# Spreading the reciprocal RMS by two DMAs through DRAM, and reordered scatters and stage changes, in a graph layer with a mixture of experts

## The chip, the cores and the metric

The kernel runs on one core of a Trainium2 chip. All data are 32-bit floats in and out. The metric is the device time of the whole program in microseconds (us). PE is TensorE (matmuls and transposes), DVE is VectorE, ACT is ScalarE, POOL is GpSimd, and SP is the engine that here only issues DMAs and waits. Every engine works through its own list of instructions strictly in order, and the engines wait for each other through semaphores.

## The reference

There are 8192 tokens (128 graphs of 64 nodes) of width 128. The first layer aggregates over a graph, the second is a mixture of 8 experts of which each token uses 2:

```
x = x + gnn(layernorm(x), adj)
    agg = epsilon * h + adj @ h
    z   = agg @ W1 + b1                       # 128 -> 512
    z   = silu(z * rsqrt(mean(z*z) + 1e-6) * rms_weight)
    out = z @ W2 + b2                         # 512 -> 128
x = x + ffn(layernorm(x))
    logits = h @ Wg + bg; the two largest, softmax over the two
    out = sum over the two experts e of  w_e * (gelu(h @ W1[e] + b1[e]) @ W2[e] + b2[e])
```

## The kernel before

The work has two stages. The **first stage** goes over 16 groups (G) of 512 tokens, each with its tokens along the free dimension in four pieces (JT = 4) of 128. In its step s PE multiplies group s by W1 (first_layer, L600), adds the skip path (residual, L607) and multiplies by W2 (second_layer, L614), and between these it does work for groups ahead: agg for group s+3 (aggregate, L566), and a quadratic form that gives the mean square of z without computing z (quadratic, L574, the product on DVE, L851, and sum_squares, L582). The mean square of group s+1 leaves DVE (mean_square, L855) at the start of step s, and POOL raises it to the power -1/2 together with two variances (pow_step, L435). The result has one token per partition, four columns. Agg has a feature per partition and tokens along the free dimension. So PE transposes the four columns, each broadcast to 128 columns, into a PSUM bank (spread, L592), where each token's factor then stands in all 128 partitions, and DVE multiplies agg by that bank (scale_agg, L861) in the same step s, ahead of the first layer of group s+1.

DVE also takes the results of the step before out of PSUM (take_x2, L867), makes the second layer norm's statistics, the gate's logits, the two best experts (gate_scores to gate_choice, L890 to L912) and, from prefix sums that PE makes (prefix, L623 to L628), the row of each token in a table per expert (rank_rows, place_rows, L921 to L937). POOL scatters the tokens' rows into these tables in DRAM with one indirect DMA per 128 tokens and choice (dispatch, L446): 64 for the first choices, 64 for the second.

The **second stage** goes over 142 tiles of 128 slots, 71 of first choices and then 71 of second choices. SP loads a tile's rows into a ring of 16 buffers once the tile 16 places earlier has been written (load_slots, L358), DVE normalises it (norm_slots, L1052) and copies its expert's first-layer block (copy_block, L1046), PE transposes it and does both layers (turn, layer1, layer2, L686, L693, L708), ACT does the Gelu (L797), DVE adds bias and weight (finish, L1121), and POOL writes the rows to their tokens: plain writes for first choices (L458), accumulating ones for second choices (L461). The scatters that are left from the first stage stand between the writes on POOL. SP also writes 16 blocks of padding rows (pad, L351), each after reading its place from a table.

The order on every engine is written out by hand. PE's order in a step and DVE's around the changed part are:

```
first_layer(s); residual(s,0); residual(s,1); second_layer(s,0); spread(s+1)          # PE
second_layer(s,1); ...; quadratic(s+2); ...; prefix(s-1); aggregate(s+3); sum_squares(s+2)
take_x2(s-1); stats2_of; moments2_of; mean_square(s+1); norm1(s+3); place_adj(s+4)    # DVE
stats1_of(s+5); gate_scores(s-1); gate_top; scale_agg(s+1); gate_index; gate_choice
product(s+2); rank_rows(s-1); place_rows(s-1)
```

## Time and profile before

| | us |
|---|---|
| median of 3 runs | 490.04 (488.69 to 491.08) |
| the profiled execution, whole | 489.22 |
| its span, first to last instruction | 487.3 |
| PE busy | 468.2 |
| POOL busy | 357.5 |
| DVE busy | 352.8 |
| ACT busy | 263.5 |

The span is what the profile covers; the whole execution has about 1.9 us around it. A busy time is the sum of an engine's instructions; issuing a DMA from SP or waiting is not counted. A timeline row gives start and duration in us, engine, source line, operation, tiles as out<-in with shapes, the number of merged instructions, and in brackets the engine's idle time before the row and what ended it; "issue" means that nothing which the profile shows was waited for. The first stage ends at about 199 us: the last matmuls of its 16th step start at 198.77.

### The profile page before, as it was taken

Reading aid. Unit: us, or ns where it says so; the run is one execution under the profiler, and the core shown is the slowest. Engines: PE = TensorE matmul, PEld = TensorE weight load, DVE = VectorE, ACT = ScalarE, POOL = GpSimd, SP = SyncE. Lnnn points to the kernel's source line nnn. Section 1 sums busy time; section 2 is a strip of 40 time slices with the busy share of each in tenths; the row PEclk is TensorE's granted clock in tenths of the full one; section 3 lists DMA queues with packets and bytes.
Section 4 is the critical chain, followed back from the end, with each engine's and each line's share of the span. In section 5 each row is a group of like instructions: output and inputs, shape, how many; then the busy total and the mean of one; then the engine's idle time right before and its main releaser. Section 6 shows DMA issues by size and latency. Waiting matters only on the chain. (4 is left out here: it accounts for less than half of the span.)

```text
span 487.3 us, 14189 instructions
## 1 busy us (share of the span) xinstructions
PE 468.2 (96%) x3715; PEld 423.1 (87%) x3715; DVE 352.8 (72%) x1476; ACT 263.5 (54%) x829; POOL 357.5 (73%) x318
## 2 busy tenths in 40 slices
PE   8999999999999999799999899999999999999990
PEld 5687888877888877799999799999999999999990
DVE  6788888887887675698866576766767676776751
ACT  2333333333333324477777577777777777777770
POOL 4622577787877777777777777777588888888884
PEclk9999999999999999999999999999999999999997
DMA  5995122222222212332343343333254555555430
GB/s 178 363 316 178 57 72 79 73 77 62 67 68 65 78 45 65 84 80 85 97 113 107 97 112 86 86 89 91 44 69 68 73 72 73 72 69 71 55 33 6
DMA packets 54436, 44.78 MB, mean 92 GB/s; under 512 B 9506, under 2 KB 46024, under 8 KB 54360
## 3 DMA queue, kind: packets, MB, share of 16 engines
q1 hardware_dynamic: 36480, 26.11, 20.3%
q0 software_dynamic: 16592, 17.13, 17.5%
q8 instruction: 35, 0.57, 0.5%
q10 hardware_dynamic: 1288, 0.62, 0.5%
q14 instruction: 41, 0.34, 0.3%
HBM read 25.49 MB, written 19.25 MB: 92 GB/s over the span
## 5 line engine op out<-in xcount | busy, mean ns | idle before, releaser
L797 ACT ACTIVATE gelu_t<-ps,block_w 128x128 f32<-128x128 f32 x568 | 162.0, 368 | 35.9 <-PE ps L693 35.4
L446 POOL DMA_INDIRECT dispatched_rows<-payload,row_idx x128 | 124.9, 976 | 37.4 <-issue 35.9
L693 PE MATMUL ps<-slot_t,block_w 128*128 128x128 f32 x1136 | 150.7, 275 | 0.9 <-ACT gelu_t L797 0.4
L708 PE MATMUL ps<-experts,gelu_t 128*128 x1136 | 150.4, 275 | 0.4 <-ACT gelu_t L797 0.4
L693 PEld LDWEIGHTS ps<-slot_t,block_w 128*128 128x128 f32 x1136 | 138.1, 192 | 1.9 <-issue 0.8
L708 PEld LDWEIGHTS ps<-experts,gelu_t 128*128 128x128 f32 x1136 | 138.2, 192 | 0.8 <-issue 0.8
L461 POOL DMA_INDIRECT out_y<-y_out,slot_rows x71 | 112.6, 1585 | 24.6 <-issue 24.6
L458 POOL DMA_INDIRECT out_y<-y_out,slot_rows x71 | 72.0, 1015 | 23.7 <-issue 18.8
L1121 DVE TENSOR_TENSOR y_bias<-ps,block_w 128x128 f32<-128x128 f32 x142 | 41.4, 291 | 65.3 <-PE ps L708 63.5
L1046 DVE COPY block_w<-experts 128x644 f32 x142 | 73.0, 514 | 1.3 <-issue 1.3
L614 PE MATMUL ps<-w2e,hidden 128*128 128x136 f32 x512 | 69.6, 279 | 0.0
L1052 DVE TENSOR_SCALAR slot_n<-slot_rows 128x128 f32<-128x128 f32 x142 | 58.6, 414 | 8.1 <-DMA slot_rows<-dispatched_rows 7.9
L614 PEld LDWEIGHTS ps<-w2e,hidden 128*128 128x128 f32 x512 | 63.9, 190 | 0.0
L757 ACT ACTIVATE hidden<-ps,vec_cols 128x512 f32<-128x512 f32 x64 | 44.0, 687 | 32.8 <-PE ps L600 32.7
L791 ACT COPY slot_t<-ps 128x128 f32<-128x128 f32 x142 | 37.6, 265 | 40.7 <-PE ps L686 40.2
L600 PE MATMUL ps<-agg_r,w1b 128*128 128x512 f32 x128 | 59.1, 603 | 0.0
L435 POOL TENSOR_TENSOR powers<-powers_in,neg_half 128x12 f32<-128x12 f32 (+2 forms) x17 | 33.8, 1985 | 23.3 <-DVE powers_in L855 22.1
L600 PEld LDWEIGHTS ps<-agg_r,w1b 128*128 128x128 f32 x128 | 23.0, 190 | 22.6 <-issue 22.5
L686 PE MATMUL ps<-ident,slot_n 128*128 128x128 f32 x142 | 38.9, 275 | 3.3 <-DVE slot_n L1052 3.3
L770 ACT ACTIVATE agg<-ps,ones 128x512 f32<-128x512 f32 x16 | 11.0, 687 | 52.4 <-PE ps L566 52.4
L1131 DVE TENSOR_SCALAR y_out<-y_bias,slot_rows 128x128 f32<-128x128 f32 x71 | 31.1, 438 | 2.5
L607 PEld LDWEIGHTS ps<-ident_wg,xs_t 128*128 128x128 f32 x128 | 20.5, 190 | 13.9 <-issue 13.9
(146 smaller groups left out, 416.7 us busy)
## 6 DMA issues: line engine op xcount, KB each, us to landing
slot_rows<-dispatched_rows SPq DMA_DIRECT2D x142, 66.5 KB
xs<-in_x SPq DMA_DIRECT2D x16, 256.0 KB, 5.9
xs_t<-in_x_t SPq DMA_DIRECT2D x16, 256.0 KB, 3.1
experts<-in_f_w SPq DMA_DIRECT2D x16, 256.0 KB, 5.2
out_y<-y_out,slot_rows POOLq DMA_INDIRECT x142, 3.2
adj_in<-in_adj_t SPq DMA_DIRECT2D x16, 128.0 KB, 4.3
dispatched_rows<-payload,row_idx POOLq DMA_INDIRECT x128, 2.5
dispatched_rows<-pad_rows SPq DMA_DIRECT2D x18, 66.5 KB
```

The source lines that it names most:

```text
L446: pool.indirect_dma_start(rows[k], bass.IndirectOffsetOnAxis(row_idx[:, g, j * TOP_K + k:j * TOP_K + k + 1], 0), payload[:, g * JT + j, 0: ...
L458: pool.indirect_dma_start(out, token, y_out[:, r, :], None, bounds_check=T - 1, oob_is_err=False).then_inc(added[r], 16)
L461: pool.indirect_dma_start(out, token, y_out[:, r, :], None, bounds_check=T - 1, oob_is_err=False, compute_op=ALU.add).then_inc(added[r], 16)
L600: pe.matmul(bank(n % H_BANKS, 0, GROUP), w1b[:, c * P:(c + 1) * P], agg_r[:, s % 2, :], start=True, stop=True).then_inc(h_done, 1)
L614: mm = pe.matmul(x2_part(j), hidden[:, c, j * P:(j + 1) * P], w2e[:, c, :], start=False, stop=(c == C - 1))
L693: mm = pe.matmul(bank((2 * i + c // 2) % FH_BANKS, c % 2 * SLOTS, SLOTS), block_w[:, i % BLOCKS, c * P:(c + 1) * P], slot_t[:, i % 2, :], ...
L708: mm = pe.matmul(bank(Y_BANK + i % 2, 0, P), gelu_t[:, i % 2, c, :], experts[:, bass.ds(at + (OW2 + c * P), P)], start=(c == 0), stop=(c = ...
L757: act.activation(hidden[:, c, :], ps[:, (C * s + c) % H_BANKS, :], ACT.Silu, scale=vec_cols[:, GRW + c:GRW + c + 1]).then_inc(hidden_ready, 1)
L797: act.activation(gelu_t[:, i % 2, c, :], ps[:, (2 * i + c // 2) % FH_BANKS, c % 2 * SLOTS:(c % 2 + 1) * SLOTS], ACT.Gelu, bias=block_w[:, ...
L1046: dve.tensor_copy(block_w[:, i % BLOCKS, :], experts[:, bass.ds(at, OW2)]).then_inc(block_ready, 1)
L1052: dve.tensor_scalar(slot_n[:, i % (AHEAD + 1), :], row[:, X2:WID], row[:, MEAN:MEAN + 1], row[:, RSTD:RSTD + 1], ALU.subtract, ALU.mult).t ...
L1121: dve.tensor_tensor(y_bias[:, i % 2, :], ps[:, Y_BANK + i % 2, 0:P], block_w[:, i % BLOCKS, OB2:OB2 + P], ALU.add).then_inc(y_chain, 1)
```

## The change

1. For groups 3 to 15 PE's spread is gone. SP, once the powers are there, stores the four columns (128 partitions x 16 B) in a 2 KB row in DRAM, waits for it, and loads that row into all 128 partitions of `rrms_all` (a part of the tile y_out, which the first stage does not use otherwise). scale_agg then reads both operands from SBUF, the factors with a stride of four elements. PE's quadratic form from group 4 on waits for the product before it instead of for the scaled agg.
2. Second choices on POOL: 2 or 3 in turn per step of the first stage instead of 3, and 3 per five tiles of the second stage instead of 2.
3. POOL no longer waits for all written tiles in one place ahead of the accumulating part, but for two at a time from tile 63 on.
4. The padding blocks on SP: 8 over the last 16 early tiles (every second one), 8 over later tiles (every third), instead of 16 on 16 consecutive tiles.
5. The first four adjacency blocks are placed by DVE instead of POOL.
6. At the end of the first stage DVE normalises two tiles and copies one expert's block earlier, and ACT loads the Gelu table in step 15.
7. ACT's first two DMAs change places.

```diff
+        rrms_all = y_out[:, 2 * JT:, :].rearrange("p (b j) q -> p b (j q)", b=2)
...
-        SECONDS_LEFT = 3 * (G + 1 - SECONDS_FROM)
+        def second_of(s):
+            return (5 * (s - SECONDS_FROM) + 1) // 2
+        SECONDS_LEFT = second_of(G + 1)
...
+            def spread(g):
+                sp.wait_ge(agg_r_ready, g - 1)
+                sp.wait_ge(powers_ready, g)
+                sp.dma_start(rrms_rows[g % 2].rearrange("(p j) -> p j", j=JT),
+                             powers[:, g - 1, 0, :]).then_inc(rrms_stored, 16)
+                sp.wait_ge(rrms_stored, 16 * (g - SPREAD_FROM + 1))
+                sp.dma_start(rrms_all[:, g % 2, :],
+                             rrms_rows[g % 2:g % 2 + 1, :].to_broadcast([P, GROUP])).then_inc(rrms_spread, 16)
+
             for g in range(XT_RING, G):
+                if g - 3 >= SPREAD_FROM:
+                    spread(g - 3)
...
             for i in range(RING, EARLY):
                 load_slots(i)
-                if i == EARLY - KE:
+                if i == EARLY - 2 * E:
                     sp.wait_ge(ends_ready, 1)
-                if i >= EARLY - KE:
-                    pad(i - (EARLY - KE))
+                if i >= EARLY - 2 * E and i % 2 == 0:
+                    pad((i - (EARLY - 2 * E)) // 2)
...
             for i in range(EARLY, TILES):
                 load_slots(i)
+                if i % 3 == 0 and (i - EARLY) // 3 < E:
+                    pad(E + (i - EARLY) // 3)
+            sp.wait_ge(padded, 16 * (KE + TOP_K))
...
-                n = SECONDS_LEFT + (i - 1) // 5 * 2 + (i % 5 == 3)
-                if i % 5 in (1, 3) and n < G * JT:
+                n = SECONDS_LEFT + i // 5 * 3 + i % 5 // 2
+                if i % 5 in (0, 2, 4) and n < G * JT:
                     second(n)
+                if TILES - 8 <= i < TILES - 1:
+                    wait_written(2 * i - TILES)
+                    wait_written(2 * i - TILES + 1)
                 if i == TILES:
-                    for q in range(RING):
-                        pool.wait_ge(added[q], 16 * len(range(q, TILES, RING)))
+                    wait_written(TILES - 2)
+                    wait_written(TILES - 1)
...
-                if g > 1:
+                if 1 < g <= SPREAD_FROM:
                     pe.wait_ge(agg_r_ready, g)
+                if g > SPREAD_FROM:
+                    pe.wait_ge(prod_ready, g)
...
-                if live(s + 1):
+                if s + 1 < SPREAD_FROM:
                     spread(s + 1)
...
+                if s == G - 1:
+                    act.activation(table_warm[:], ones[:, 0:1], ACT.Gelu)
...
+                    dve.wait_ge(rrms_spread, 16 * (g - SPREAD_FROM + 1))
+                    dve.tensor_tensor(agg_r[:, g % 2, :].rearrange("p (j q) -> p j q", j=JT),
+                                      agg[:, g % 3, :].rearrange("p (j q) -> p j q", j=JT),
+                                      rrms_all[:, g % 2, :].rearrange("p (q j) -> p j q", j=JT),
+                                      ALU.mult).then_inc(agg_r_ready, 1)
...
+            place_adj(0)
             norm1(0)
...
+                if s == G - 1:
+                    norm_slots(0)
+                    norm_slots(1)
...
+                if s == G - 2:
+                    copy_block(0, first_at)
                 if s == G - 1:
-                    copy_block(0, expert_of(dve, 0))
-                    copy_block(1, expert_of(dve, 1))
-                    copy_block(2, expert_of(dve, 2))
-                    for i in range(AHEAD):
-                        norm_slots(i)
+                    copy_block(1, second_at)
+                    norm_slots(2)
+                    norm_slots(3)
+                    copy_block(2, third_at)
```

Where instructions stand now. SP in the steps of the first stage, before: one load of adj and one of xs_t a step.

```order
L320 DMA xs_t<-in_x_t 128x512 [waits l2_done]
L317 DMA adj_in<-in_adj_t 128x256 [waits adj_ready]
L320 DMA xs_t<-in_x_t 128x512 [waits l2_done]
L317 DMA adj_in<-in_adj_t 128x256 [waits adj_ready]
L320 DMA xs_t<-in_x_t 128x512 [waits l2_done]
```

SP in the same place now (rrms_rows is the row in DRAM; y_out stands for its part rrms_all):

```order
L313 DMA adj_in<-in_adj_t 128x256 [waits adj_ready]
L316 DMA xs_t<-in_x_t 128x512 [waits l2_done]
L339 DMA rrms_rows<-powers 128x4 [waits powers_ready,agg_r_ready]
L342 DMA y_out<-rrms_rows 128x512 [waits rrms_stored]
L313 DMA adj_in<-in_adj_t 128x256 [waits adj_ready]
L316 DMA xs_t<-in_x_t 128x512 [waits l2_done]
```

Each step has got two DMAs ahead of its loads, the second behind a wait for the first.

DVE in a step, from the top values to the prefix sums, before:

```order
L898 MAX top_vals<-logits 128x8 x3
L861 TENSOR_TENSOR agg_r<-agg,ps 128x512 [waits h_done,spread_done,gate_chain]
L903 MAX_INDEX top_idx<-top_vals,logits 128x8 x4
L907 TENSOR_TENSOR gap<-top_vals 128x4 [waits gate_chain]
L909 CAST top_no<-top_idx 128x8
L912 TENSOR_TENSOR chosen<-top_no,expert_no 128x4x8 [waits gate_chain]
L912 TENSOR_TENSOR chosen<-top_no,expert_no 128x4x8
L851 TENSOR_TENSOR prod<-agg,ps 128x512 [waits ms_done,q_done]
L921 TENSOR_TENSOR row_cand<-ps,next_row 128x64 [waits prefix_done]
```

DVE in the same place now:

```order
L920 MAX top_vals<-logits 128x8 x3
L881 TENSOR_TENSOR agg_r<-agg,y_out 128x512 [waits rrms_spread,h_done,gate_chain]
L925 MAX_INDEX top_idx<-top_vals,logits 128x8 x4
L929 TENSOR_TENSOR gap<-top_vals 128x4 [waits gate_chain]
L931 CAST top_no<-top_idx 128x8
L934 TENSOR_TENSOR chosen<-top_no,expert_no 128x4x8 [waits gate_chain]
L934 TENSOR_TENSOR chosen<-top_no,expert_no 128x4x8
L866 TENSOR_TENSOR prod<-agg,ps 128x512 [waits ms_done,q_done]
L943 TENSOR_TENSOR row_cand<-ps,next_row 128x64 [waits prefix_done]
```

The order is the same. The scaling of agg waits for rrms_spread, the landing of SP's second DMA, where it waited for PE's spread_done.

POOL from the last steps of the first stage into the first tiles (L435 powers, L446 scatters, L458 writes), before:

```order
L435 TENSOR_TENSOR powers<-powers_in,neg_half 128x8
L446 DMA dispatched_rows<-payload,row_idx 66688x133 x7
L435 TENSOR_TENSOR powers<-powers_in,neg_half 128x4
L446 DMA dispatched_rows<-payload,row_idx 66688x133 x10
L435 TENSOR_TENSOR powers<-powers_in,neg_half 128x4
L446 DMA dispatched_rows<-payload,row_idx 66688x133 x4
L458 DMA out_y<-y_out,slot_rows 8192x128
L446 DMA dispatched_rows<-payload,row_idx 66688x133
L458 DMA out_y<-y_out,slot_rows 8192x128 x2
L446 DMA dispatched_rows<-payload,row_idx 66688x133
L458 DMA out_y<-y_out,slot_rows 8192x128 x3
L446 DMA dispatched_rows<-payload,row_idx 66688x133
```

POOL in the same place now (L443 powers, L454 scatters, L466 writes):

```order
L443 TENSOR_TENSOR powers<-powers_in,neg_half 128x8
L454 DMA dispatched_rows<-payload,row_idx 66688x133 x6
L443 TENSOR_TENSOR powers<-powers_in,neg_half 128x4
L454 DMA dispatched_rows<-payload,row_idx 66688x133 x10
L443 TENSOR_TENSOR powers<-powers_in,neg_half 128x4
L454 DMA dispatched_rows<-payload,row_idx 66688x133 x4
L466 DMA out_y<-y_out,slot_rows 8192x128 x2
L454 DMA dispatched_rows<-payload,row_idx 66688x133
L466 DMA out_y<-y_out,slot_rows 8192x128 x2
L454 DMA dispatched_rows<-payload,row_idx 66688x133
L466 DMA out_y<-y_out,slot_rows 8192x128
L454 DMA dispatched_rows<-payload,row_idx 66688x133
```

A step in the middle has 6 or 7 scatters where it had 7, and among the first tiles three scatters stand for every five writes, where it was two.

## Rows read from the trace of the kernel before

**Rows 1.** The page, part 1 and part 2: PE's busy time and granted clock.
```profile
PE 468.2 (96%) x3715; PEld 423.1 (87%) x3715; DVE 352.8 (72%) x1476; ACT 263.5 (54%) x829; POOL 357.5 (73%) x318
PEclk9999999999999999999999999999999999999997
```

**Rows 2.** The stretches of 10 us, all engines, columns as in the heading row.
```profile
core 0: us, PE busy (x) PEld busy (x) DVE busy (x) ACT busy (x) POOL busy (x), PEclk, DMA share, GB/s
110.00:120.00 10.00, 10.00 (x72) 8.03 (x71) 8.67 (x46) 3.44 (x5) 8.16 (x7) 1.00 0.24 69
270.00:280.00 10.00, 8.13 (x61) 6.99 (x61) 5.10 (x16) 4.96 (x18) 7.57 (x8) 1.00 0.38 99
```

**Rows 3.** Timeline, PE, the transposes of one step and what follows.
```profile
106.66 0.60 PE L592 MATMUL ps<-ident,powers 128*128 128x128 f32 x4
107.10 1.09 PE L614 MATMUL ps<-w2e,hidden 128*128 128x136 f32 x8
```

**Rows 4.** Timeline, DVE and POOL: one step, and two other takings of x2.
```profile
44.01 0.43 DVE L867 TENSOR_TENSOR payload<-ps,b_all 128x272 f32<-128x272 f32 x1
...
101.22 0.78 DVE L867 TENSOR_TENSOR payload<-ps,b_all 128x272 f32<-128x272 f32 x2
...
103.68 2.33 POOL L435 TENSOR_TENSOR powers<-powers_in,neg_half 128x12 f32<-128x12 f32 x1 [0.26 <-DVE powers_in L855]
...
107.66 0.69 DVE L861 TENSOR_TENSOR agg_r<-agg,ps 128x512 f32<-128x512 f32 x1
...
109.22 0.29 DVE L912 TENSOR_TENSOR chosen<-top_no,expert_no 128x32 bf16<-128x32 f32 x2
...
111.59 0.23 DVE L921 TENSOR_TENSOR row_cand<-ps,next_row 128x64 f32<-128x64 f32 x1 [0.66 <-PE ps L628]
...
112.72 0.78 DVE L867 TENSOR_TENSOR payload<-ps,b_all 128x272 f32<-128x272 f32 x2
...
169.88 0.43 DVE L867 TENSOR_TENSOR payload<-ps,b_all 128x272 f32<-128x272 f32 x1
```

**Rows 5.** Landings of xs_t; SP's issue of the last pad and its wait.
```profile
DMA to landing us min/median/max: 2.8/3.0/3.6
...
273.38 0.36 SPq L351 DMA_DIRECT2D dispatched_rows<-pad_rows  x1
...
SPq L356 <- DMA dispatched_rows<-pad_rows: 2.2, 1, 2.2
```

**Rows 6.** Timeline, DVE and POOL, the start.
```profile
7.03 2.60 DVE L837 TENSOR_SCALAR xn<-xs,mv,rstd 128x128 f32<-128x128 f32 x4 [1.16 <-POOL rstd L411]
7.23 3.12 POOL L273 TENSOR_TENSOR adj_blocks<-adj_in,eps_ident 64x256 f32<-64x256 f32 x4 [0.23 <-POOL rstd L411]
...
12.95 1.11 DVE L837 TENSOR_SCALAR xn<-xs,mv,rstd 128x128 f32<-128x128 f32 x4 [1.20 <-POOL rstd L411]
```

**Rows 7.** PE at the stage change; DVE's waits for slots (sum, times, longest).
```profile
200.74 0.49 PE L686 MATMUL ps<-ident,slot_n 128*128 128x128 f32 x2 [1.73 <-DVE slot_n L1052]
...
DVE slot_n L1052 <- DMA slot_rows<-dispatched_rows: 7.9, 7, 1.8
```

**Rows 8.** Second stage: DVE's first result, POOL's timeline, the page's group and landing.
```profile
205.79 0.29 DVE L1121 TENSOR_TENSOR y_bias<-ps,block_w 128x128 f32<-128x128 f32 x1 [1.97 <-PE ps L708]
...
209.31 1.08 POOL L435 TENSOR_TENSOR powers<-powers_in,neg_half 128x4 f32<-128x4 f32 x1 [1.16 <-DVE powers_in L884]
...
215.85 1.00 POOL L458 DMA_INDIRECT out_y<-y_out,slot_rows  x1 [0.30 <-issue]
...
341.93 0.98 POOL L458 DMA_INDIRECT out_y<-y_out,slot_rows  x1 [0.92 <-DVE y_out L1128]
...
343.82 0.98 POOL L458 DMA_INDIRECT out_y<-y_out,slot_rows  x1 [0.92 <-DVE y_out L1128]
...
348.02 1.57 POOL L461 DMA_INDIRECT out_y<-y_out,slot_rows  x1 [3.22 <-issue]
...
L461 POOL DMA_INDIRECT out_y<-y_out,slot_rows x71 | 112.6, 1585 | 24.6 <-issue 24.6
...
out_y<-y_out,slot_rows POOLq DMA_INDIRECT x142, 3.2
```

More of the change, by code:

```diff
@@ L66, in moe_gnn @@
     GRW, GB2, FB1 = 0, C, C + 1
-    XT_RING, ADJ_RING, PLACED = 4, 8, 4
+    XT_RING, ADJ_RING = 4, 8
     AHEAD = 4
@@ L202, in moe_gnn @@
         eps_ready = sem("eps_ready")
+        clear_chain = sem("clear_chain")
         ln1_chain = sem("ln1_chain")
@@ L220, in moe_gnn @@
         spread_done = sem("spread_done")
+        rrms_stored = sem("rrms_stored")
+        rrms_spread = sem("rrms_spread")
         agg_r_ready = sem("agg_r_ready")
@@ L261, in live @@
             return 0 <= g < G
-        def wait_adj(engine, g):
-            if g < PLACED:
-                engine.wait_ge(adj_placed, g + 1)
-            else:
-                engine.wait_ge(adj_ready, g - PLACED + 1)
-        def half_of_adj(engine, g, h):
-            half = slice(h * NODES, (h + 1) * NODES)
-            return engine.tensor_tensor(
-                adj_blocks[half, g % 4, :, half], adj_in[half, g % ADJ_RING, :, :],
-                eps_ident[half, half].rearrange("p (a n) -> p a n", a=1).to_broadcast([NODES, JT, NODES]),
-                ALU.add)
         def after(engine, semaphore, value):
@@ L359, in load_slots @@
                              rows[i // TILES][bass.ds(first, SLOTS), :]).then_inc(slots_loaded[r], 16)
+            spread(G - 3)
+            spread(G - 2)
             sp.wait_ge(early_table_ready, 1)
@@ L372, in _ @@
                 load_slots(i)
+                if i == 0:
+                    spread(G - 1)
             for i in range(RING, EARLY):
                 load_slots(i)
-                if i == EARLY - KE:
+                if i == EARLY - 2 * E:
                     sp.wait_ge(ends_ready, 1)
-                if i >= EARLY - KE:
-                    pad(i - (EARLY - KE))
+                if i >= EARLY - 2 * E and i % 2 == 0:
+                    pad((i - (EARLY - 2 * E)) // 2)
             sp.wait_ge(tables_ready, 1)
-            sp.wait_ge(padded, 16 * (KE + TOP_K))
+            sp.wait_ge(padded, 16 * (E + TOP_K))
             sp.wait_ge(late_dispatched, 16 * JT * (G - EARLY_GROUPS))
@@ L493, in _ @@
                 if s >= SECONDS_FROM:
-                    second(3 * (s - SECONDS_FROM))
+                    second(second_of(s))
                 if s == G:
@@ L500, in _ @@
                 if s >= SECONDS_FROM:
-                    second(3 * (s - SECONDS_FROM) + 1)
-                    second(3 * (s - SECONDS_FROM) + 2)
+                    second(second_of(s) + 1)
+                    if second_of(s) + 2 < second_of(s + 1):
+                        second(second_of(s) + 2)
             for i in range(NT):
@@ L562, in aggregate @@
                 pe.wait_ge(xn_ready, g + 1)
-                wait_adj(pe, g)
+                pe.wait_ge(adj_ready, g + 1)
                 after(pe, agg_copied, g)
@@ L844, in place_adj @@
                 for h in range(P // NODES):
-                    m = half_of_adj(dve, g, h)
+                    half = slice(h * NODES, (h + 1) * NODES)
+                    m = dve.tensor_tensor(
+                        adj_blocks[half, g % 4, :, half], adj_in[half, g % ADJ_RING, :, :],
+                        eps_ident[half, half].rearrange("p (a n) -> p a n", a=1).to_broadcast([NODES, JT, NODES]),
+                        ALU.add)
                 m.then_inc(adj_ready, 1)
@@ L858, in scale_agg @@
             def scale_agg(g):
-                dve.wait_ge(spread_done, g + 1)
                 after(dve, h_done, C * (g - 1))
-                dve.tensor_tensor(agg_r[:, g % 2, :], agg[:, g % 3, :], ps[:, QR_BANK, :],
-                                  ALU.mult).then_inc(agg_r_ready, 1)
+                if g < SPREAD_FROM:
+                    dve.wait_ge(spread_done, g + 1)
+                    dve.tensor_tensor(agg_r[:, g % 2, :], agg[:, g % 3, :], ps[:, QR_BANK, :],
+                                      ALU.mult).then_inc(agg_r_ready, 1)
+                else:
+                    dve.wait_ge(rrms_spread, 16 * (g - SPREAD_FROM + 1))
+                    dve.tensor_tensor(agg_r[:, g % 2, :].rearrange("p (j q) -> p j q", j=JT),
+                                      agg[:, g % 3, :].rearrange("p (j q) -> p j q", j=JT),
+                                      rrms_all[:, g % 2, :].rearrange("p (q j) -> p j q", j=JT),
+                                      ALU.mult).then_inc(agg_r_ready, 1)
             def take_x2(g):
@@ L1053, in norm_slots @@
                                   ALU.subtract, ALU.mult).then_inc(slots_normed, 1)
-            dve.memset(adj_blocks[:], 0.0).then_inc(adj_clear, 1)
+            clear = Chain(dve, clear_chain)
+            clear.link(dve.memset(adj_blocks[:], 0.0))
             stats1_of(0)
+            dve.wait_ge(eps_ready, 1)
+            place_adj(0)
             norm1(0)
@@ L1059, in _ @@
             stats1_of(1)
+            place_adj(1)
             norm1(1)
@@ L1068, in _ @@
             stats1_of(2)
-            stats1_of(3)
+            place_adj(2)
             norm1(2)
             setup_w2()
+            stats1_of(3)
+            place_adj(3)
             norm1(3)
```

33 lines of the change are left out of this document (9 added, 24 removed).

## The prediction

> **What bounds the kernel now.** I began with the page: PE is busy for 96% of the span at a granted clock of nine tenths or more everywhere but at the very end [rows 1], so anything that shortens PE's list can help, if nothing else becomes late. Next came the stretches of 10 us: in the first stage and in most of the second PE has no idle time at the full clock; one exception is 270 to 280 us, with 8.13 of 10 us busy [rows 2]. Then I laid out one step of the first stage in order of time, PE [rows 3] and DVE with POOL [rows 4]. The reader is to see a loop in [rows 4]: DVE takes x2 out of PSUM (101.22), makes the mean square, POOL raises it to the power (103.68 to 106.01), and in the same step DVE scales agg by it (107.66) and only then makes the choice of experts (109.22), waits for the prefix sums of PE (111.59), and takes the next x2 (112.72). DVE works strictly in its written order. A step takes 11.44 us on the mean: (169.88 - 44.01) / 11 [rows 4]. PE fills it: in a stretch of 10 us there it is busy for 10.00 [rows 2], and it has nothing to wait for.
>
> **What the new path of the reciprocal RMS costs.** Removed from PE: four transposes in each of 13 steps (groups 3 to 15). They hold PE from 106.66 to 107.10 [rows 3], 0.44 us, so PE needs 11.0 us a step instead of 11.44 and could give back 13 x 0.44 = 5.7 us. Added on SP: a DMA of 128 x 16 B to DRAM, its wait, and a DMA of 256 KB back. The scaling on DVE stays where it was in DVE's list, between the top values and the index search, and now waits for the second landing. Its operands change from PSUM to SBUF with a stride; I take its 0.69 us as unchanged (bounds 0.6 and 1.4, a doubling), since the row has one operand in SBUF already.
>
> Nothing in the trace is this pair of DMAs. The nearest to the first is a store of 66.5 KB from SBUF to DRAM by the same queue: issued at 273.38 with 0.36 us of issue, then SP waited 2.2 us for it [rows 5], so 2.6 us from issue to landing. It moves more bytes, but the new one has as many pieces, each of 16 B; I take 2.6, bounds 2.1 and 3.6. The nearest to the second is the load of xs_t, also 128 x 2 KB: 2.8 to 3.6, median 3.0 us [rows 5]; I take 3.0, bounds 2.8 and 3.6 (all 128 pieces read the same 2 KB of DRAM). With about 0.1 us for the second hand-over, L = 5.7 us, bounds 5.0 and 7.3. The Trainium skill (DMA: Bandwidth & Descriptors, Anatomy of one DMA) gives each DMA about 2.0 us fixed, mostly the receipt of the write, plus bytes over 436 GB/s; so going by DRAM pays the receipt twice, which speaks against the change. By it the pair would take 2.0 + 2.0 + 0.6 = 4.6 us, an estimate, the step 13.1 and the whole run 515; the trace is slower than the rule (3.0 against its 2.6 for xs_t [rows 5]).
>
> The loop then reads, with rows of [rows 4]: from taking x2 (101.22) to the end of the power (106.01) 4.79; L 5.7; from the start of the scaling (107.66) to the end of the choice (109.22 + 0.29) 1.85; the product of the next group but one 0.7, beside which PE makes the prefix sums; from the ranks (111.59) to the next x2 (112.72) 1.13. Together 8.47 + 5.7 = 14.2 us, against 11.44: **+2.73 us a step**. Already hidden in this are 1.6 us between 106.01 and 107.66, where DVE has statistics and gate scores to do; the other 4.1 us are a bare stall of DVE. Behind the waiting instruction stand the index search, the choice, the product and the ranks. PE waits for the choice before its prefix sums: 14.2 - 11.0, so 3.2 us of idle time a step appear on an engine that had none. POOL gets slack in this stage. SP has nothing late behind its waits: the loads of adj and xs_t are needed steps later, and the queue is past the experts' loads by then. 13 steps give 13 x 2.73 = **+35.5 us** (bounds: 13 x 2.0 and 13 x 4.3, so +26 and +56; I stay near the lower half because both measured landings have their medians near their lower ends).
>
> **The start.** Placing the first four adjacency blocks moves from POOL to DVE. The first normalisation on DVE took 2.60 us beside POOL's placing of blocks, the next, with POOL idle, 1.11 us [rows 6], so 1.5 us of contention goes, and placing a block fits in the 1.16 us that DVE waits for POOL ahead of it. PE was filled there partly with idle matmuls, so not all comes through: **-1 us**, bounds -2 and +1 (four times 0.85 us more on DVE if nothing hides it would be later than that, but DVE has waits there).
>
> **The stage change.** PE waits 1.73 us for the first slots [rows 7]; with the blocks copied ahead, two slots normalised ahead and the Gelu table loaded ahead, these 1.7 us and perhaps one more go from PE. This is worth nothing at the end if POOL decides, which is the next point.
>
> **The second stage.** POOL's list decides here. A scatter or write costs it 1.00 + 0.30 = 1.30 us, as at 215.85, its first write. That write comes 10 us after the first tile left PE (205.79), and from there POOL works without a gap, catching up, until it waits for DVE at 341.93 and 343.82, one tile of 1.89 us apart, which is PE's rate [rows 8]. After the power at 209.31, before has 4 + 22 + 4 scatters and 71 writes, 101 items, ahead of the accumulating part. Now 2.5 second choices stand in a step of the first stage instead of 3, so 29 instead of 22 are left and one fewer scatter follows the power in the last step: 107 items. (The moved ones leave a stage in which POOL will be waiting anyway.) Tile 70 would then start about 106 x 1.30 = 138 us after the power, against 343.82 - 210.4 = 133.4, so +4.4. The power itself comes perhaps 0.4 us sooner. The waits for landed writes are now spread: that for tile 68 stands one item behind its write, which lands 3.2 us after its issue (the page's median), so 3.2 - 1.3 = +1.9; the 14 waits less between 343.82 and 348.02 give 0.4 back. Sum 4.4 - 0.4 + 1.9 - 0.4 = **+5.5 us**, bounds 0 and +8. From there on POOL accumulates one tile in 1.585 + 0.30 = 1.89 us [rows 8], PE's own rate, so this lag stays to the end. Half of the pads leaving SP's list before tile 40 removes seven waits of DVE for slots, 7.9 us [rows 7], which cost PE the 1.9 us of [rows 2] and some more; I count this at nothing since POOL is behind PE at that point, and at -4 if POOL were not.
>
> **Sum.** The profiled execution took 489.2 us (span 487.3 and 1.9 around it). 489.2 + 35.5 - 1 + 5.5 = 529.2. The median of the runs is 0.8 higher: **530 us**.
>
> **Rivals.**
> (a) The DMAs are hidden. This needs L under 11.0 - 8.47 = 2.5 us; then PE bounds the step, 5.7 us go, and with -1 and +5.5 for the rest the time is 488, or 483 if POOL's list does not bind; a small gain. Against it: each of the two landings alone exceeds 2.5 us in [rows 5]. Chance 0.04 for faster, 0.02 for no change (within 0.5%, about what a measurement of this kernel tells apart).
> (b) The pair is as quick as my lower bounds in every step, 2.1 + 2.8 + 0.1 = 5.0: step 13.5, 13 x 2.03 = 26, time 520. For it: 16 B a piece is little to move. Against it: the median landing of xs_t is 3.0 us, and the store's only row says 2.6. Chance 0.14.
> (c) The clock falls. PE had its full clock through both stages, with a gap of 1.73 us the longest I saw [rows 1, 7]; now it has 3.2 us idle in every step. If the granted clock went to its lower level, 1.2 GHz, for half of each step, PE would need 16.5 us, 2.3 more than the DVE loop gives it: 13 x 2.3 = 30 more, 560 us. For it: the gap is longer than any in the trace. Against it: no row at all shows a fall in the first stage, and the first 3 us of loss fall into PE's own idle time. Chance 0.07. The Trainium skill (TensorE: Matmul & The Clock Gate, HAM oscillation) warns that repeated idle gaps of PE throw the clock down again and again; no row of this trace tests it.
> (d) The forecast as summed, chance 0.73.
>
> **How the numbers follow.** (b), (c) and (d) are slower: 0.94. Low end: L at its lower bound, POOL's term at -4 and the start at -2, 489.2 + 26 - 4 - 2 + 0.8 = 510. High end: L near 6.5 (13 x 3.5 = 46) and POOL's +8 gives 543, with part of (c) 549. The range is 510 to 549.
>
> **What would show it.** Right: steps of about 14.2 us between two takings of x2; DVE idle some 4 us before agg_r with the DMA into rrms_all (the y_out tile) as its releaser; PE idle about 3 us before the matmuls with chosen; no L592 transposes beyond three groups; stage two beginning some 35 us later; POOL's first accumulating write some 5 us later relative to the stage's start. Wrong: steps of 11 us (the DMAs hidden), a granted clock under 1.00 in the first stage, or steps longer than 16 us, which would say that one of the two DMAs takes far longer than the rows I compared it with.

## The result, and the profile after

| | before | changed |
|---|---|---|
| time, median of runs | 490.6 us (488.7 to 491.1, 4 runs) | 547.1 us (545.8 to 548.9, 4 runs) |
| ratio | | 1.116 (95% interval 1.112 to 1.120) |
| span of the profiled execution | 487.3 us | 544.3 us |
| mean granted clock of TensorE | 0.993 | 0.936 |

Slower by 57 us, inside the range (510 to 549) and on the side that was forecast, but 17 us above the forecast of 530. The page of the changed kernel shows where: PE has lost its nines in the first half of the span, and its granted clock with them.

```profile
PE 492.4 (90%) x3663; PEld 432.6 (79%) x3663; DVE 357.1 (66%) x1484; ACT 264.2 (49%) x830; POOL 359.4 (66%) x310
PEclk9999796978979797899999999999999999999995
```

Against [rows 1], every engine is busy for the same time within about 5%; the 57 us are mostly waiting. PE's 24 us more are matmuls at a lower clock, as is shown below under the clock. Three of the stretches of 10 us answer to [rows 2] (the value behind the stretch's length is PE's busy time, the third from the end the granted clock): full work at the full clock, PE with idle time, and PE busy throughout at a lower clock.

```profile
70.00:80.00 10.00, 9.83 (x70) 7.71 (x69) 8.89 (x54) 3.74 (x7) 6.10 (x5) 1.00 0.19 50
110.00:120.00 10.00, 6.17 (x44) 5.49 (x43) 4.95 (x27) 0.75 (x3) 5.59 (x5) 0.82 0.40 109
150.00:160.00 10.00, 10.00 (x34) 6.17 (x35) 5.41 (x31) 3.42 (x5) 6.86 (x6) 0.63 0.27 50
```

The timeline of one step, with rows of POOL, SP, DVE and PE, answers to [rows 3, 4]:

```profile
134.60 0.78 DVE L889 TENSOR_TENSOR payload<-ps,b_all 128x272 f32<-128x272 f32 x2
137.06 2.33 POOL L443 TENSOR_TENSOR powers<-powers_in,neg_half 128x12 f32<-128x12 f32 x1 [4.36 <-DVE powers_in L870]
139.46 0.33 SPq L339 DMA_DIRECT2D rrms_rows<-powers  x1
140.63 0.37 DVE L920 MAX8 top_vals<-logits 128x8 f32<-128x8 f32 x4
140.87 0.33 SPq L342 DMA_DIRECT2D y_out<-rrms_rows  x1
145.32 1.07 DVE L881 TENSOR_TENSOR agg_r<-agg,y_out 128x512 f32<-128x512 f32 x1 [4.32 <-DMA y_out<-rrms_rows]
147.26 0.29 DVE L934 TENSOR_TENSOR chosen<-top_no,expert_no 128x32 bf16<-128x32 f32 x2
147.61 0.23 PE L630 MATMUL ps<-chosen,before 128*128 128x64 bf16 x1 [3.36 <-DVE chosen L934]
148.07 0.23 DVE L943 TENSOR_TENSOR row_cand<-ps,next_row 128x64 f32<-128x64 f32 x1
149.15 0.78 DVE L889 TENSOR_TENSOR payload<-ps,b_all 128x272 f32<-128x272 f32 x2
```

The reader is to see the loop closed by the two DMAs: the power ends at 139.39, the store is issued at 139.46, the load at 140.87, and only at 145.32 can DVE scale. DVE stood still for 4.32 us of that, and PE for 3.36 us behind it. The first and last of these takings of x2 bound 13 steps:

```profile
43.41 0.78 DVE L889 TENSOR_TENSOR payload<-ps,b_all 128x272 f32<-128x272 f32 x2
...
239.91 0.78 DVE L889 TENSOR_TENSOR payload<-ps,b_all 128x272 f32<-128x272 f32 x2
```

That is 196.5 / 13 = 15.12 us a step. Before, the same 13 ran from 44.01 [rows 4] to 191.77, 11.37 us each, so +48.7 us:

```profile
191.77 0.78 DVE L867 TENSOR_TENSOR payload<-ps,b_all 128x272 f32<-128x272 f32 x2
```

The sums of waits (engine, what waited, for what: us in total, times, longest) have the same in two lines, and one of the second stage that answers to [rows 7]:

```profile
DVE agg_r L881 <- DMA y_out<-rrms_rows: 63.8, 13, 5.5
...
DVE slot_n L1074 <- DMA slot_rows<-dispatched_rows: 27.1, 23, 2.8
```

```profile
PE ps L630 <- DVE chosen L934: 24.2, 10, 4.2
```

The 24.2 us of PE are not spread evenly. Ahead of the prefix sums PE stood 3.0 to 4.2 us in six of the 13 steps, 2.0 in one and 0.7 or less in the other six. The two kinds alternate: after each of the six long gaps the next step had none or a short one, and in the case shown the matmuls in between ran at the lower clock.

In the second stage these rows answer to [rows 7, 8]: the first turn on PE, DVE's first result, POOL's last power and first write, then tiles 68, 69 and 70 and the first accumulating write.

```profile
245.89 0.42 PE L693 MATMUL ps<-ident,slot_n 128*128 128x128 f32 x2
250.87 0.29 DVE L1154 TENSOR_TENSOR y_bias<-ps,block_w 128x128 f32<-128x128 f32 x1 [1.34 <-PE ps L715]
256.50 1.17 POOL L443 TENSOR_TENSOR powers<-powers_in,neg_half 128x4 f32<-128x4 f32 x1
263.19 1.00 POOL L466 DMA_INDIRECT out_y<-y_out,slot_rows  x1 [0.30 <-issue]
395.24 0.98 POOL L466 DMA_INDIRECT out_y<-y_out,slot_rows  x1 [0.82 <-issue]
399.94 1.25 POOL L466 DMA_INDIRECT out_y<-y_out,slot_rows  x1 [3.72 <-DVE y_out L1164]
401.49 0.98 POOL L466 DMA_INDIRECT out_y<-y_out,slot_rows  x1 [0.30 <-issue]
404.43 1.67 POOL L469 DMA_INDIRECT out_y<-y_out,slot_rows  x1 [1.96 <-DVE y_out L1164]
```

PE begins the stage 45.2 us later (200.74 before), POOL's last power stands 47.2 us later, its first accumulating write 56.4 us later (348.02 before) [rows 7, 8]. So 9.2 us are lost on POOL between the power and the accumulating part.

### The profile page after: what moved, and what is told of

Its sections match the earlier page's. It is cut to its first block and busy times, and to the rows that moved or that the text cites. A ratio compares the mean times of both kernels' runs of the same rounds, so it can differ in the third digit from the quotient of the medians.

```text
span 544.3 us, 14119 instructions
## 1 busy us (share of the span) xinstructions
PE 492.4 (90%) x3663; PEld 432.6 (79%) x3663; DVE 357.1 (66%) x1484; ACT 264.2 (49%) x830; POOL 359.4 (66%) x310
## 3 DMA queue, kind: packets, MB, share of 16 engines
q0 software_dynamic: 16592, 17.13, 15.6%
## 5 line engine op out<-in xcount | busy, mean ns | idle before, releaser
L454 POOL DMA_INDIRECT dispatched_rows<-payload,row_idx x128 | 131.2, 1025 | 37.4 <-issue 36.4
L466 POOL DMA_INDIRECT out_y<-y_out,slot_rows x71 | 72.9, 1026 | 25.6 <-issue 20.0
L443 POOL TENSOR_TENSOR powers<-powers_in,neg_half 128x12 f32<-128x12 f32 (+2 forms) x17 | 33.9, 1996 | 73.7 <-DVE powers_in L870 67.5
L607 PE MATMUL ps<-agg_r,w1b 128*128 128x512 f32 x128 | 77.0, 756 | 0.0
L1074 DVE TENSOR_SCALAR slot_n<-slot_rows 128x128 f32<-128x128 f32 x142 | 58.2, 411 | 28.2 <-DMA slot_rows<-dispatched_rows 27.1
L621 PE MATMUL ps<-w2e,hidden 128*128 128x136 f32 x512 | 67.5, 279 | 0.0
L607 PEld LDWEIGHTS ps<-agg_r,w1b 128*128 128x128 f32 x128 | 29.8, 246 | 33.0 <-issue 32.9
L881 DVE TENSOR_TENSOR agg_r<-agg,y_out 128x512 f32<-128x512 f32 x13 | 14.0, 1080 | 63.8 <-DMA y_out<-rrms_rows 63.8
L770 ACT COPY payload<-powers 128x4 f32<-128x4 f32 x16 | 3.2, 198 | 85.4 <-DVE gap L929 85.4
## 6 DMA issues: line engine op xcount, KB each, us to landing
slot_rows<-dispatched_rows SPq DMA_DIRECT2D x142, 66.5 KB
```

The lines of the kernel that those rows point to most:

```text
L454: pool.indirect_dma_start(rows[k], bass.IndirectOffsetOnAxis(row_idx[:, g, j * TOP_K + k:j * TOP_K + k + 1], 0), payload[:, g * JT + j, 0: ...
L466: pool.indirect_dma_start(out, token, y_out[:, r, :], None, bounds_check=T - 1, oob_is_err=False).then_inc(added[r], 16)
L607: pe.matmul(bank(n % H_BANKS, 0, GROUP), w1b[:, c * P:(c + 1) * P], agg_r[:, s % 2, :], start=True, stop=True).then_inc(h_done, 1)
L621: mm = pe.matmul(x2_part(j), hidden[:, c, j * P:(j + 1) * P], w2e[:, c, :], start=False, stop=(c == C - 1))
L1074: dve.tensor_scalar(slot_n[:, i % (AHEAD + 1), :], row[:, X2:WID], row[:, MEAN:MEAN + 1], row[:, RSTD:RSTD + 1], ALU.subtract, ALU.mult).t ...
```

## The experiments

Theory: DVE's wait for the second landing makes the step long, and a longer POOL list the rest. Rivals: other parts of the change slow the first stage; the transfers themselves hold it up, wherever DVE stands; the clock.

One thing must be known first. On three of the chips that these runs fell on, the kernel before takes 605 to 611 us instead of 490, and totals there say little. What is seen on them is that results of TensorE reach their readers later than its records have them, 4.8 us in rows shown below; here, such a chip is said to hold TensorE, a name and not a cause. So the experiments are told by what they can tell.

**The changed kernel again.**

> The changed kernel, unaltered, beside the kernel before on whatever chip this is. Theory (the landings set a step of about 15 us whatever the chip; where a chip holds TensorE at about 16 us a step they vanish behind it): if the kernel before takes about 605 us here, the changed one takes 600 to 609 and its steps are 15.5 to 16.3 us, if it takes 490, the changed one takes 545 to 549. Rival (the DMAs' loss comes on top of a held TensorE): more than 630 us where the kernel before takes 605.

Measured: 547.14 us against 490.01 on the same chip, ratio 1.115 (1.112 to 1.118). From 43.17 to 241.95, 13 steps of 15.3 us; the wait of DVE for the load sums to

```profile
DVE agg_r L881 <- DMA y_out<-rrms_rows: 66.0, 13, 6.3
```

The loss is the kernel's, not one chip's. What the changed kernel takes on a chip that holds TensorE stayed unmeasured.

**Undo the DMAs, or add them alone (first set).** Spread by TensorE in every step, all else as changed:

```
-        SPREAD_FROM = 3
+        SPREAD_FROM = G
```

> The changed kernel with PE's transposes kept for all 16 groups (no DMA by way of DRAM), everything else of the change kept. Theory: the DMA path costs 48.7 us in the first stage, POOL's longer list and its waits some 9 us in the second, the start gives 0.6. Then this takes 490 - 0.6 + 6 to 9 = 497 us (495 to 500), with steps of 11.44 us. Rival: the second stage only looks late because the first was disturbed, and the stage changes gain; then 486 to 489 us.

The kernel before with the DMAs alone (its `scale_agg`, `quadratic` and SP list as in the change, from group 3 on):

> The kernel before with the two DMAs for groups 3 to 15 as the only change. Theory: 490 + 48 = 538 us (535 to 541), with steps of about 15.1 us, and the second stage as long as before. Rival: the parts do not add, since PE's clock, which falls in the first stage, carries part of the loss into the second; then 543 us or more, or below 533 if POOL's slack in the first stage shortens its list in the second.

As the first, but with POOL's order of second choices and its waits for writes as before:

```
-            return (5 * (s - SECONDS_FROM) + 1) // 2
+            return 3 * (s - SECONDS_FROM)
...
-                if TILES - 8 <= i < TILES - 1:
-                    wait_written(2 * i - TILES)
...
+                    for q in range(RING):
+                        pool.wait_ge(added[q], 16 * len(range(q, TILES, RING)))
```

> PE's transposes kept, and POOL's list as before (three second choices a step, two per five tiles, one place for the waits); start, pads, stage change, Gelu table and first DMAs as in the change. Theory: POOL works without a gap from its first write to tile 67 before, so what PE gains at the stage change and by the moved pads (3 and 2 to 3 us) comes through only as far as POOL is not the bound: 487.5 us (486 to 489). Rival: these parts are worth nothing, 490 us.

As the first, with only the waits for writes as before:

> As the first of these kernels (PE's transposes kept, five second choices in two steps), but with all waits for written tiles in one place ahead of tile 71, as before. Theory: the wait for tile 68 one write behind it cost 3.7 us of idle POOL in the changed kernel, the 14 waits more cost 0.4; so this is 2 to 3 us quicker than the first kernel, about 494.5 us. Rival: the wait is only moved, since tile 70 must land anyway; then it is within 1 us of the first kernel.

Measured: 602.4, 606.0, 603.3 and 602.8 us, where the kernel before took 605.0 (ratios 0.998, 1.001, 0.997 and 0.996, intervals of 0.003 either way or less). Every expectation in microseconds missed, by 65 to 116, and the ratios cannot tell theory from rival. Steps were 15.6 us in the first and 16.0 in the second (ten steps, from 55.02 and 60.72 on). With the DMAs alone the total was that of the kernel before, here and in the next set (1.001 both times): on such a chip they cost nothing that shows in it.

**The same two again.**

> The changed kernel with one part taken back: the factors are spread by TensorE's four transposes in every step, as before. Repeated because in the first runs the chip held every kernel, the one before too, at 600 to 606 us. Theory (the two DMAs and the scaling behind them are what costs in the first stage): steps fall from 15.1 to 11.2 to 11.5 us, the stage change comes near 197 us in the profile instead of 241, and the time is 495 to 500 us if the kernel before takes 490, the rest over 490 being the later part of the program. Rival (the stage change or the two-step choice slow the first stage themselves): steps of 12 us or more and a time above 505.

> The kernel before with the two DMAs alone added from group 3 on (its own order, POOL's list and choices kept). Repeated on the ground given for the first. Theory: steps of 15.0 to 15.3 us as in the changed kernel, so 13 times 3.7 = 48 us over the kernel before: 536 to 541 us if that takes 490. Rival (the reworked stage change or the choice in two steps carries part of the loss of the first stage): under 532; (they had hidden part of it): over 544.

Measured, on another chip of that kind: 602.4 and 605.4 us against 605.3. The trace of the first shows what is different there, in the fourth step (PE's prefix and aggregation, then DVE and ACT that wait for them):

```profile
64.97 0.24 PE L631 MATMUL ps<-chosen,ones_bf 128*128 128x16 bf16 x4
65.07 1.14 PE L567 MATMUL ps<-adj_blocks,xn 128*128 128x128 f32 x8
70.04 0.22 DVE L939 TENSOR_TENSOR row_cand<-ps,next_row 128x64 f32<-128x64 f32 x1 [3.66 <-remote]
70.13 0.69 ACT L773 ACTIVATE agg<-ps,ones 128x512 f32<-128x512 f32 x1 [6.89 <-remote]
```

Both results were ready at 65.2 and 66.2 by PE's records, whose ends are modelled, and both readers started at 70.0 and 70.1. Without the DMAs such a halt recurs in every second step, every 31 us, and makes the loop nearly as long as the DMAs do. Only the step ahead of the first such halt is clean. It is the first with a spread by DMA: 14.55 us (45.58 to 60.13) with the DMAs against 11.87 us (43.16 to 55.03) without, and in the first set 14.75 against 11.93. In each pair the DMAs alone put 2.7 or 2.8 us on a step. That is one step; it bears the theory out and no more.

**Distinct rows.** The second DMA reads 128 rows of an input instead of one row 128 times; the factors are then input values, not the reciprocal RMS.

```
-                              rrms_rows[g % 2:g % 2 + 1, :].to_broadcast([P, GROUP])).then_inc(rrms_spread, 16)
+                              x_t[:, g * GROUP:(g + 1) * GROUP]).then_inc(rrms_spread, 16)
```

> The changed kernel, but the second DMA reads 128 different rows of 2 KB of an input (256 KB from 256 KB) instead of one row of 2 KB 128 times. The factors in the scaling are then input values, not the reciprocal RMS. Theory (the load takes 4.5 us from issue to the scaling where such a load of the inputs takes 3.1, because all its descriptors read one row): the load falls to about 3.2 us, a step to about 13.8, the time by 13 times 1.3 = 17 us to 528 to 532. Rival (the load is slow because of what runs beside it, POOL's scatters and the experts' loads): it stays at 4.3 us or more and the time within 3 us of the changed kernel's.

Measured: 604.6 us, no use as a time on this chip. The landing is not hidden by what TensorE does: from issue to scaling 3.70 us on the mean of 13 (3.0 to 4.7), against 4.38 (4.0 to 5.2) for the single row in the run with the DMAs alone on the same chip. So reading one row costs 0.7 us of the load, about half of its excess over 3.0; neither expectation held in full, 3.2 nor 4.3. The other half was there with distinct rows too; what it comes from (POOL's scatters, the experts' loads) was not separated.

**Scaling one step later.** VectorE scales group s behind the take of x2 in step s, when its factors should have landed long ago.

```
                     take_x2(s - 1)
+                    if s >= SPREAD_FROM:
+                        scale_agg(s)
                     stats2_of(s - 1)
...
-                if live(s + 1):
+                if s + 1 < SPREAD_FROM:
                     scale_agg(s + 1)
```

> The changed kernel with the scaling of a group put one step later on VectorE, behind the next group's take of the second layer, so that nothing on VectorE waits for the loads; everything that is computed stays. Theory (the loss is VectorE standing still for the landing, not the bytes or the queues): VectorE's waits for the load go from 63.8 us to under 5, the steps to 11.4 to 12.0 us, the time to 495 to 508 us if the kernel before takes 490. Rival (the transfers themselves, or TensorE with its first layer put off by one step, hold the step up): steps of 13 us or more, time over 520.

Measured: 615.9 us against 605.3, ratio 1.017 (1.012 to 1.023), on the chip that holds TensorE; steps 16.5 us (ten steps, 54.81 to 220.06). DVE's waits for the load are gone, as expected, and PE now waits for the scaling, 17.6 us in 13 times. The time is 10.5 us over that of the kernel before; that PE's new wait makes it is likely but not shown. Steps over 13 us are what the rival forecast, but on this chip the steps are about 16 us in every uncut kernel, so they decide nothing. What the later scaling does elsewhere was left to the last run.

**Less work for TensorE.** To take the held engine off the bound, of the four products of each second layer only the last is made, in both stages.

```
-                for c in range(C):
+                for c in range(C - 1, C):
```

> The kernel before with less work on TensorE: of the four products of each second layer only the last is made, in both stages (the output is then not the reference's). It is the ground for the next run. The chips of the two earlier sets held every kernel at about 605 us, with TensorE's results up to 4 us behind their records once POOL's writes had begun, so steps were 16 us with and without the DMAs. Theory (TensorE's held rate is the bound there; cut to about 70% of its work it no longer is): steps fall to 11.0 to 12.5 us. Rival (the hold is not a matter of how much TensorE has to do): steps stay above 14.

> The same cut in the kernel before with the two DMAs alone added from group 3 on. Theory (the two DMAs put 3.7 us on a step as soon as TensorE isn't the bound): steps of 14.5 to 15.2 us, the stage change 40 to 50 us later than in the kernel with the same cut and without the DMAs, and the time 38 to 50 us longer. Rival (the landings are hidden, and the loss of the changed kernel came from its other parts): steps within 0.5 us of the other's and the time within 6 us.

Measured: 558.0 us (the median of three runs; a fourth, 569.6 us, is left out) and 586.9 us, with 611.2 for the kernel before on this chip. The steps are 12.96 us without the DMAs (65.58 to 169.26, 8 steps; the last ones before the stage change are 13.7 to 15.5) and 15.47 with them (57.07 to 196.31, 9 steps); over the 13 steps with a spread by DMA the means are 13.11 and 15.28. In the profiled executions, with spans of 555.5 and 588.3 us, PE begins the second stage at 222.6 and 249.7: 27.1 us of the 32.8 us between them arise in the first stage, and the other 5.7 in the second, where the two kernels do not differ. The rival (hidden, within 6 us) falls. The size missed, 28.9 for 38 to 50, because the step without the DMAs did not come down to 11.4: even so cut, TensorE's results were late (ACT's wait for the aggregation, laid to no engine, is 67.9 us in 10). With the DMAs the step is as long as in the changed kernel, 15.5 for 15.1 and 15.3 us, though TensorE has far less to do: it is set by the loop. DVE in the second of the two:

```profile
DVE agg_r L889 <- DMA y_out<-rrms_rows: 58.3, 12, 5.3
```

**Late scaling, contiguous factors, less work for TensorE.** The later scaling and the cut of above, and the factors are read in the order in which they lie (they reach other tokens):

```
-                                      rrms_all[:, g % 2, :].rearrange("p (q j) -> p j q", j=JT),
+                                      rrms_all[:, g % 2, :].rearrange("p (j q) -> p j q", j=JT),
```

> The changed kernel with TensorE's second layers cut to the last of their four products as in the two runs before, and two edits to the scaling: it stands one step later on VectorE, behind the next take of the second layer, and it reads the factors in contiguous order instead of at a stride of four words (the factors then reach other tokens). Theory (a step is long because VectorE stands waiting for the load, and the stride makes the scaling 1.08 instead of 0.69 us): no wait of VectorE for the load, scaling 0.68 to 0.75 us, steps 12.5 to 13.5 us against 15.3 with the DMAs and 12.95 without them, and 555 to 565 us in all. Rival (the bytes of the load or TensorE's later first layer hold the step up too): steps above 14.5; (the 1.08 us come from where the factors lie in SBUF and not from the stride): the scaling stays above 1.0.

This one fell on the chip of the repeated changed kernel (490.0 for before, 547.1 for the changed one) and took 494.5 us, so the expected times and steps, made for a chip that holds TensorE, are off by 60 us and 1 to 2 us. DVE waits 9.0 us for the load, in 8 of 13 steps, instead of 66.0; none was expected. The scaling takes 0.69 us. A step (the same rows as above) and the start of the next:

```profile
121.63 0.78 DVE L889 TENSOR_TENSOR payload<-ps,b_all 128x272 f32<-128x272 f32 x2
122.33 0.68 DVE L881 TENSOR_TENSOR agg_r<-agg,y_out 128x512 f32<-128x512 f32 x1
...
123.06 3.70 PE L607 MATMUL ps<-agg_r,w1b 128*128 128x512 f32 x8 [0.76 <-DVE agg_r L881]
...
124.56 2.33 POOL L443 TENSOR_TENSOR powers<-powers_in,neg_half 128x12 f32<-128x12 f32 x1 [1.55 <-DVE powers_in L870]
...
126.97 0.32 SPq L339 DMA_DIRECT2D rrms_rows<-powers  x1
...
128.37 0.32 SPq L342 DMA_DIRECT2D y_out<-rrms_rows  x1
...
129.50 0.29 DVE L934 TENSOR_TENSOR chosen<-top_no,expert_no 128x32 bf16<-128x32 f32 x2
...
131.37 0.78 DVE L889 TENSOR_TENSOR payload<-ps,b_all 128x272 f32<-128x272 f32 x2
...
133.36 0.69 DVE L881 TENSOR_TENSOR agg_r<-agg,y_out 128x512 f32<-128x512 f32 x1 [1.21 <-DMA y_out<-rrms_rows]
...
134.10 6.59 PE L607 MATMUL ps<-agg_r,w1b 128*128 128x512 f32 x8 [2.08 <-DVE agg_r L881]
```

Both DMAs are there and no quicker (load 5.0 us from issue to use), but the choice comes at 129.50 without waiting for them. Twelve steps take 11.39 us each on the mean (42.14 to 178.83), and PE begins the second stage at 199.18 instead of 247.93. The rival that the transfers themselves, or a later first layer, hold the step up falls in the size it had, steps above 14.5. A part of it stays. The steps are uneven, 9.3 to 14.1 us; in the one that begins at 131.37, of 13.95 us, DVE still stood 1.21 us for the load, PE 2.08 us for the scaling, and the first layer then took 6.59 us at a granted clock of 0.66 (130 to 140). And 11.39 is not the least that TensorE's cut load allows: the step ahead of the first DMAs takes 10.12 us here (32.02 to 42.14; 10.13 in the same place of the kernel before with the cut load), so with the later scaling the two DMAs still cost some 1.3 us a step. That 11.39 is also the step of the uncut kernel before is chance.

TensorE's cut load alone is not what shortened the step: the pair before had the same cut, and 15.47 us with the DMAs where DVE waits, though on a chip of the other kind. The stride makes 0.39 us of the difference. A run on this kind of chip with the early scaling and the cut load, or with the later scaling and the full load, is missing. So whether the full load fits 11.4 us with the later scaling stays open, since PE waits for the scaling here, 22.0 us in 13 times, and at full load it has no such time to spare. The rival on the place in SBUF falls too: same place, no stride, 0.69 us, where the run with the later scaling and the stride had 1.05.

The second stage of this run took 493.9 - 199.2 = 294.7 us with six of the seventeen matmuls of a tile left out, against 545.2 - 247.9 = 297.3 in the changed kernel on the same chip. So TensorE's work does not set its length, though its granted clock was lower there too (0.87 to 1.00, in stretches of 50 us from 200 to 450); this fits POOL as the bound. POOL's list itself was undone only where TensorE was held, so its price is read from the traces and not tested. The same holds for the DMAs: no run takes them alone out of the changed kernel where TensorE is not held.

No version beats the kernel before beyond doubt. Where TensorE was held, the spread by transposes with the rest of the change took 0.995 and 0.998 of its time (intervals 0.991 to 0.998 and 0.996 to 0.9997); on the other kind of chip it was not run.

## Why the prediction was right, and where it was off

- **The loop and its sign: right.** DVE idle before the scaling with the landing as releaser, forecast 4.1 us, 4.9 on the mean (63.8 / 13). PE idle ahead of the prefix sums, forecast about 3 us in every step: over 3 us in six of the 13, 1.9 on the mean (24.2 / 13), since the lower clock used up the rest. The last run takes away most of DVE's wait and not the DMAs, and the steps fall to 11.4, with TensorE's load cut as well.
- **The removed transposes:** nothing, as the loop sets the step and not PE.
- **L, forecast 5.7 us, bounds 5.0 to 7.3: measured 6.30.** Its two parts were off in opposite ways. Store: issue to the load's issue 1.4 us in nine of 13 steps, mean 1.70, forecast 2.6, so under its lower bound of 2.1; its nearest row had 66.5 KB, and SP's wait in it was for the last of many stores. Load: 4.52 to the scaling, forecast 3.0 with 3.6 as the upper bound, so this bound was broken in 12 of 13 steps. I had named that all pieces read the same 2 KB and priced it at nothing. The Trainium skill (DMA: Bandwidth & Descriptors, Anatomy of one DMA) gives about 2.0 us fixed and, as an estimate from its formula, 2.6 for the load: above the measured store of 1.4, and 1.9 below the load. That section's formula is fitted to DMAs issued from GpSimd, and these are issued from SP, which the prediction did not say.
- **The scaling, forecast unchanged at 0.69: 1.08 us**, inside its bounds. The late scaling has 1.05 us with the stride and 0.69 without it, so the stride makes it. 0.39 us in 13 steps, 5 us.
- **The step.** 8.47 + 6.30 + 0.39 = 15.16; measured 15.12, forecast 14.2. That these meet to 0.04 is partly luck. Read from the changed kernel's rows, the same terms of an undisturbed step are 4.79 + 6.29 + 2.23 + 0.52 + 1.07 = 14.90; the prediction's 8.47 is 0.24 too long. The mean is above that because the ranks came late in four steps: by 0.3 and 0.7 us behind matmuls at the lower clock, and by 1.2 and 1.9 us in the last two, where DVE has work of the stage change between the choice and the ranks (the 1.9 with the block copy that the change moved there). The powers of the last three steps, 0.65 us shorter each, give 2.0 us back. So +48.7 us for 13 steps, forecast +35.5 (bounds +26 and +56). These 13.2 us are most of the miss: 7.8 from L, 5.1 from the scaling.
- **The start:** forecast -1, measured -0.6.
- **The stage change:** PE gained 3.0 us there (48.1 at the takings of x2, 45.2 at the first turn), forecast 1.7 to 2.7, and as forecast it was worth nothing at the end; POOL's power gained 0.9.
- **The second stage, forecast +5.5 us with bounds 0 and +8: measured +8.9**, over the bound. From the power to the first accumulating write 147.9 us instead of 138.7, +9.2. From the first write to tile 68 (395.24; before 340.03) POOL had 32 scatters instead of 26 and took 132.05 us for 124.18, +7.9 at 1.32 us an item in both; the six items more were foreseen, but my 4.4 put 1.30 an item for the new list against a measured stretch of the old one that had 1.33. Tile 69 followed tile 68 after 4.70 us instead of 1.90, +2.8 for a forecast of +1.9, and 1.6 came back by the first accumulating write. The reordered pads were to remove DVE's seven waits for slots (7.9 us); there are 23 of them instead, 27.1 us. That step of the prediction failed, and its cause was not looked for. PE is down to 45.50 of 50 us busy from 300 to 350, 4.5 us that I had valued at nothing; POOL was behind PE, so this holds.
- **The range.** 547.1 lies 2 us under its upper end, 549. That end took L at 6.5 and not at its own upper bound of 7.3, and had no term for the scaling; with them the range would have been wider.
- **Rival (c), the clock,** had 0.07 at 560 us. The clock did fall, to between 0.63 and 0.93 in 13 of the 20 stretches of 10 us from 40 to 240, which the prediction had listed as a sign of being wrong, though it cost far less than the 30 us named. After PE had stood 3.36 us (147.61), the granted clock is 0.63 over 150 to 160, a mix of 2.4 and 1.2 GHz, and the first layer takes 6.68 us instead of 3.68:

```profile
151.30 6.68 PE L607 MATMUL ps<-agg_r,w1b 128*128 128x512 f32 x8
```

But the loop leaves PE most of the time: PE went from one step's prefix sums (147.61) to the next's (163.31) without a gap, 15.7 us, where the loop needs 14.9, and the ranks came 0.7 us late. In one other step they came 0.3 us late by this, and in four the power came 0.1 us late. The Trainium skill (TensorE: Matmul & The Clock Gate, HAM oscillation) warned of the fall, and this trace shows it. What it costs depended here on which engine set the step.

## What to carry to other kernels

A transfer by way of DRAM is cheap only where nothing in a strictly ordered list stands waiting for it. Here it took 6 us; with the consumer in the same step the loop grew by 3.7 us, and with the consumer one step later, and less work on TensorE, a step took 11.4 us on the mean, some 1.3 over the same load without the DMAs. Before moving work off the busiest engine, lay out the loop that runs through all engines: 0.44 us of PE was bought with 4.9 us of DVE. And price a broadcast read and a strided operand from a row of that form, or give them their own bounds.

## What was not expected of the hardware

- A store of 128 x 16 B from SBUF to DRAM is seen by the waiting queue 1.4 us after its issue (9 of 13; mean 1.70, highest 2.86).
- A load of 128 x 2 KB takes 4.4 to 4.5 us from issue to its use when all read one row of DRAM, 3.7 with distinct rows (means of 13; 4.38 and 3.70 on the same chip).
- A 128 x 512 product of two f32 operands in SBUF takes 0.69 us, and 1.08 with one of them at a stride of four words.
- Three chips held TensorE: 605.0, 605.3 and 611.2 us for a kernel that takes 490.0 on others. From some 60 us on, results came late against PE's records (4.8 us in the rows shown), every 31 us in the first stage without the DMAs, and the mean clock of the uncut kernels was 0.89 to 0.93; but from 500 to 550 us PE ran at its full rate, 451 matmuls in 50 us, as many as before had from 350 to 400 us on the other kind. Cutting TensorE's work took 53 us from the whole and did not end it. What causes it stays open.
